# The first feed-forward stage of an eight-stage kernel as one scheduled block, with masks turned by DMA

## The reference

```python
INTER, SPARSITY, RANK = 1792, 32, 16
inter = xf @ c1_w.T @ c2_w.T                  # c1_w [16, 512], c2_w [1792, 16]
blk = inter.reshape(B * T, INTER // SPARSITY, SPARSITY)
idx = jnp.argmax(blk, axis=-1) + jnp.arange(0, INTER, SPARSITY)
h = jax.nn.relu(jnp.einsum('bkm,bm->bk', w1[idx], xf))
out = jnp.einsum('bk,bkm->bm', h, w2t[idx])
x = x + out
```

## Time and profile before

| | |
|---|---|
| median of 3 runs | 1888.47 us (1884.77 to 1889.16) |
| profiled execution | 1886.01 us, span 1884.3 us |
| granted TensorE clock, mean | 0.929 of full speed |
| PE busy | 1605.5 us (85%) |
| DVE busy | 1178.5 us (63%) |
| ACT busy | 796.8 us (42%) |
| POOL busy | 608.8 us (32%) |

### The profile page before, as it was taken

One profiled execution on the slowest core, in us unless ns is written; L12 is line 12 of the kernel. 1 busy time (PEld: TensorE's weight loads), 2 busy tenths in 40 slices (PEclk: granted clock), 3 DMA queues, 4 the chain that ended last, 5 costly groups with the idle time before them and its releaser, 6 DMA issues. The chain is left out here.

```text
span 1884.3 us, 31640 instructions
## 1 busy us (share of the span) xinstructions
PE 1605.5 (85%) x10796; PEld 897.1 (48%) x10796; DVE 1178.5 (63%) x2287; ACT 796.8 (42%) x2789; POOL 608.8 (32%) x517
## 2 busy tenths in 40 slices
PE   2888955899899999996699999999996769449997
PEld 1455532344366666652365555555552334234443
DVE  5677776434455555564588887888777879771212
ACT  2676755211044334332176666666652312251111
POOL 2333328100014443450066666666653001220000
PEclk9899976799999999998799999999999779869998
DMA  2000012000034442240264546565433000200001
GB/s 103 15 15 15 1 69 92 0 0 0 1 83 93 78 78 62 57 79 26 94 141 104 132 106 129 105 133 107 99 77 91 34 1 1 62 31 0 0 0 45
DMA packets 265956, 111.07 MB, mean 59 GB/s; under 512 B 232305, under 2 KB 248497, under 8 KB 265698
## 3 DMA queue, kind: packets, MB, share of 16 engines
q1 hardware_dynamic: 265826, 109.40, 25.1%
HBM read 52.74 MB, written 2.10 MB: 29 GB/s over the span
## 5 line engine op out<-in xcount | busy, mean ns | idle before, releaser
L67 PE MATMUL bank<-a_wo_hi,a_o_hi 128*128 128x512 f16 (+1 forms) x416 | 159.1, 382 | 19.1 <-DVE a_o_lo L824 10.4
L1443 POOL TENSOR_TENSOR a_recip<-a_total,minus_one 128x4 f32<-128x4 f32 x96 | 97.8, 1019 | 195.9 <-ACT a_probs L1295 195.9
L69 PE MATMUL bank<-a_wo_hi,a_o_lo 128*128 128x512 f16 (+1 forms) x416 | 159.1, 383 | 0.0
L68 PE MATMUL bank<-a_wo_lo,a_o_hi 128*128 128x512 f16 (+1 forms) x416 | 159.1, 382 | 0.0
L1450 POOL TENSOR_TENSOR a_normal<-a_probs,a_recip 128x512 f32<-128x512 f32 x128 | 155.4, 1224 | 7.5
L1435 POOL TENSOR_TENSOR a_q_ss<-a_q_ss,half 128x4 f32<-128x4 f32 x64 | 89.2, 1393 | 189.3 <-DVE a_q_ss L1365 95.5
L1295 ACT ACTIVATE a_probs<-a_masked,a_negmax 128x128 f32<-128x128 f32 x256 | 99.6, 390 | 94.8 <-DVE a_negmax L1340 94.8
L1306 ACT ACTIVATE a_o_hi<-bank 128x512 f16<-128x512 f32 (+1 forms) x96 | 57.1, 595 | 180.6 <-PE bank L69 180.4
L1558 ACT ACTIVATE f_h_hi<-f_h 128x512 f16<-128x512 f32 (+1 forms) x50 | 31.5, 630 | 205.8 <-DVE f_h L1579 144.1
L67 PE MATMUL bank<-xn_hi,f_w_hi 128*128 (+1 forms) x288 | 110.9, 385 | 8.2 <-PEq L1511 8.2
L437 POOL TENSOR_TENSOR a_kb_lo<-a_k_lo,a_spread 128x1024 f16<-128x1024 f16 x32 | 69.4, 2169 | 150.1 <-PE bank L69 139.5
(11 more groups left out here) (338 smaller groups left out, 4894.4 us busy)
## 6 DMA issues: line engine op xcount, KB each, us to landing
a_nq<-in_L_xattn_Wq SPq DMA_DIRECT2D x8, 1024.0 KB, 5.7
a_no<-in_L_xattn_Wo SPq DMA_DIRECT2D x8, 1024.0 KB, 6.0
f_n<-in_L_ffn_w SPq DMA_DIRECT2D x1, 3584.0 KB, 11.6
f_n<-in_L_ffn_w2t SPq DMA_DIRECT2D x1, 3584.0 KB, 20.2
a_nq<-in_L_xattn_Wq SPq DMA_DIRECT2D x4, 768.0 KB, 4.8
a_no<-in_L_xattn_Wo SPq DMA_DIRECT2D x4, 768.0 KB, 5.7
f_words<-in_L_ffn_w SPq DMA_DIRECT2D x2, 1280.0 KB, 6.0
ctx_nat<-in_ctx_t SPq DMA_DIRECT2D x4, 512.0 KB, 4.9
```

What stands on the lines that cost most here:

```text
L67: pe.matmul(out, lh, rh, start=start, stop=False)
L68: pe.matmul(out, lh, rl, start=False, stop=False)
L69: return pe.matmul(out, ll, rh, start=False, stop=stop)
L1443: pool.tensor_tensor(recip[s % 2][:, :], total[s % 2][:, :], K.minus_one[:, :], ALU.pow).then_inc(recip_done.sem, 1)
```

## The change

`top_of_blocks_ffn` and its call of `ffn` are replaced by `blocks_ffn`, one block in which all engines follow one table of steps, -16 to 29. Step t has tile t up (0 to 27) and tile t-2 down (`LAG = 2`). All is written out; there is no loop at run time. Four tables say at which step a piece is made: `NORM` (a batch normalised), `CX` (a batch compressed), `PICK` (a batch's scores chosen, in spans of four tiles) and `SPLIT` (a weight piece of two tiles split).

- The scores come in parts of 512 units (the last of each batch has 256) and are chosen between the tiles. For the first half of the tokens, span 0 is chosen at steps -7 to -4, span 1 at -1 to 2, span 2 at 3 to 6, span 3 at 7 to 10. The first tile of a span waits for its four masks.
- Masks are turned by DMA (`turn_mask`) and no longer by PE and ACT. The rows of the layer norm are split first (DVE high, POOL low) and turned by two DMAs for each batch (`turn_rows`).
- The weights are loaded and split in 14 pieces of 512 KB; two pieces of each matrix are in flight.
- `before` has -1 on its diagonal, so that its product with the mask is -1 at the winner and not below zero elsewhere. ACT makes the gate `first_f` from it by one Relu with scale -1; the DVE operation of line 1574 is gone.
- The `up`, `side`, score and compress products take turns in a ring of four banks.

```diff
+    PARTS, HT, PIECES, TILES = -(-NT // SPAN), HALF * P, NT // 2, 2 * NT
+    FIRST, LAG, RING, MASKS = -16, 2, 2, 4
+    NORM = {0: -16, 1: -15, 2: -14, 3: -13, 4: 2, 5: 3, 6: 4, 7: 5}
+    CX = {0: -9, 1: -8, 2: -7, 3: -6, 4: 4, 5: 5, 6: 6, 7: 7}
+    PICK = {(b, i): (4 * i - 5 if i else -7) + b if b < HALF else 4 * (i + 1) + b for b in range(B) for i in range(PARTS)}
+    SPLIT = {("w1", 0): -15, ("w2", 0): -10, ("w1", 1): -6, ("w2", 1): -4}
+    SPLIT.update({(kind, q): 2 * q - 4 + i for q in range(2, PIECES) for i, kind in enumerate(("w1", "w2"))})
...
             @block.sync
             def _(sp):
...
+                def turn_rows(b):
+                    sp.wait_ge(xlo_done.sem, xlo_done.count(b))
+                    for a, dst in enumerate((K.xn_hi, K.xn_lo)):
+                        sp.dma_start_transpose(dst[:, :, b * P:(b + 1) * P], xn_hl[b % HALF][:, a, :]).then_inc(xt_in[b], 16)
+
+                def turn_mask(part):
+                    b, i = part
+                    m, n = parts.index(part) % MASKS, width(part)
+                    sp.wait_ge(pick_done.sem, pick_done.count(part))
+                    sp.dma_start_transpose(mask_t[:, SPAN * i:SPAN * i + n // P, b * P:(b + 1) * P], mask[m][:, 0:n]).then_inc(mask_in[m], 16)
...
+                for t in steps:
+                    for b in at(NORM, t):
+                        turn_rows(b)
+                    for part in at(PICK, t):
+                        turn_mask(part)
+                    for kind, q in at(SPLIT, t + 3):
+                        if q:
+                            load((kind, q))
...
             @block.tensor
             def _(pe):
...
+                for t in steps:
+                    for u in live(t):
+                        up(u)
+                        first_of_block(u)
+                    for part in at(PICK, t):
+                        score(part)
+                    for b in at(CX, t):
+                        compress(b)
+                    for u in live(t - LAG):
+                        down(u)
...
             @block.scalar
             def _(act):
...
+                    for u in live(t):
+                        first_winner(u)
+                        high_of_hidden(u)
+                    for use in at(SPLIT, t):
+                        high_of_weight(use)
+                    for b in at(CX, t):
+                        high_of_compressed(b)
...
+                def choose(part):
...
+                    dve.tensor_reduce(best, s, AX.X, ALU.max).then_inc(top_done.sem, 1)
+                    dve.wait_ge(top_done.sem, top_done.count(part))
+                    dve.tensor_tensor(dst, s, best.unsqueeze(2).to_broadcast([P, width(part) // BLK, BLK]),
+                                      ALU.is_equal).then_inc(pick_done.sem, 1)
+                    dve.wait_ge(pick_done.sem, pick_done.count(part))
+                    dve.sem_inc(ring.freed(use), 1)
...
-                with dve.Fori(1, B // 2) as p:
-                    choose(2 * p, 0)
-                    choose(2 * p + 1, 1)
-        staged.close()
-        ffn(K, L, w1_p, w2_p, first_of=(mask_t, before), keep_stats=True)
...
+                    for u in live(t):
+                        hidden(u)
+                        low_of_hidden(u)
+                    for b in at(NORM, t):
+                        normalise(b)
...
+                    for b in at(CX, t):
+                        low_of_compressed(b)
+                    for part in at(PICK, t):
+                        choose(part)
```

More of the change, by code:

```diff
@@ L1714, in top_of_blocks_ffn @@
[L1714 to L1722 removed]
+        ring_of = lambda n, k, shape, dt: [sb(f"{n}{i}", shape, dt) for i in range(k)]
@@ new lines, in blocks_ffn @@
+        live = lambda t: [t] if 0 <= t < TILES else []
+        at = lambda table, t: [use for use, when in table.items() if when == t]
+        steps = range(FIRST, TILES + LAG)
+        ring_uses = [use for t in steps
+                     for use in ([(k, u) for u in live(t) for k in ("up", "side")] + [("s", part) for part in at(PICK, t)]
+                                 + [("cx", b) for b in at(CX, t)])]
+        y_bank = Banks(K, f"{N}_y", K.bank[0:4], [(hf, n) for hf in range(2) for n in range(HALF)])
@@ new lines, in blocks_ffn @@
+        ring = Banks(K, f"{N}_ring", K.bank[4:8], ring_uses)
+        in_c, w_here = sem("in_c"), {k: [sem(f"{k}_in{i}") for i in range(RING)] for k in nat}
+        pieces = sorted(SPLIT, key=SPLIT.get)
+        whi_done, wlo_done = Steps(sem("whi"), pieces), Steps(sem("wlo"), pieces)
+        mean_done, root_done, const_done, zeroed = sem("mean"), sem("root"), sem("const"), sem("zeroed")
+        chi_done, clo_done = Steps(sem("chi"), ["c1", "c2"]), Steps(sem("clo"), ["c1", "c2"])
+        per_batch = lambda n: Steps(sem(n), batches)
@@ new lines, in blocks_ffn @@
+        xn_done, xhi_done, xlo_done, cxhi_done = (per_batch(n) for n in ("xn", "xhi", "xlo", "cxhi"))
+        parts = sorted(PICK, key=PICK.get)
+        top_done, pick_done = Steps(sem("top"), parts), Steps(sem("pick"), parts)
+        xt_in, mask_in = [sem(f"xt_in{b}") for b in batches], [sem(f"mask_in{m}") for m in range(MASKS)]
+        hhi_done, hlo_done = Steps(sem("hhi"), tiles), Steps(sem("hlo"), tiles)
+        down_done = Steps(sem("down"), [u for u in tiles if u % NT < NT - 1])
+        of_half = lambda u: range(HALF * (u // NT), HALF * (u // NT) + HALF)
@@ L1723, in _ @@
             @block.tensor
             def _(pe):
[L1725 removed]
+                for banks in (y_bank, ring):
                     for freed in banks.freed_sems:
                         pe.sem_inc(freed, 1)
[L1729 to L1734 removed]
@@ new lines, in score @@
+                def score(part):
+                    b, i = part
+                    use = ("s", part)
+                    if i == 0:
+                        pe.wait_ge(clo_done.sem, clo_done.count("c2"))
+                        pe.wait_ge(ring.freed(("cx", b)), ring.n_drained(("cx", b)))
+                    pe.wait_ge(ring.freed(use), ring.n_free(use))
+                    n, first = width(part), SPAN * P * i
+                    pe.matmul(ring[use][:, 0:n], cx_s[:, b * P:(b + 1) * P], c2_s[:, first:first + n],
+                              start=True, stop=True).then_inc(ring.filled(use), 1)
@@ new lines, in first_of_block @@
+                def first_of_block(u):
+                    f, b0, use = u % NT, HALF * (u // NT), ("side", u)
+                    if f == 0:
+                        pe.wait_ge(const_done, 4)
+                    if f % SPAN == 0:
+                        for b in of_half(u):
+                            mask_landed(pe, (b, f // SPAN))
+                    pe.wait_ge(ring.freed(use), ring.n_free(use))
+                    pe.matmul(ring[use][:, :], before[:, :], mask_t[:, f, b0 * P:b0 * P + HT], start=True, stop=True).then_inc(ring.filled(use), 1)
```

386 lines of the change are left out of this document (213 added, 173 removed).

## The result

| | before | changed |
|---|---|---|
| median | 1888.18 us (4 runs, 1884.77 to 1889.16) | 1838.63 us (4 runs, 1835.29 to 1839.53) |
| ratio to before | | 0.9739 (95%: 0.9728 to 0.9751) |
| profiled execution | 1886.01 us, span 1884.3 us | 1837.94 us, span 1836.2 us |
| PE busy | 1605.5 us (85%) | 1577.1 us (86%) |
| stage, from its first DVE instruction to that of the next | 244.39 us | 196.61 us |

What follows compares the result with a forecast made beforehand. Choosing and weight splits were taken to stand on the path ahead of PE-bound products. 303.2 + 156.1 + 2.5 = 461.8 against 512.0, 50.2 us less: 1886.0 becomes 1835.8, plus 2.5 for the median, 1838 (1829 to 1846, 0.68).

Steps and rivals of the forecast that it cites:

- The opening: Second stage up to the first tile's mask matmul: forecast at 303.2 us instead of 353.1, 49.9 us earlier.
- Done for batch 0 well before, so this is hidden by the memsets: Opening: DVE's normalisation, 0.47 us a batch plus a cast, ends before POOL's clears end at 277.7 and costs nothing.
- The mark: Start of the first tile's mask matmul, from which the prediction counts the tiles: forecast 303.2 us, before 353.1.
- 1.06 each: Opening: POOL's low halves of rows, each taken as half of 2.12 us.
- The tiles: First mask matmul to last matmul: 156.1 us of PE work plus 2.5 us of waits.
- rival 2: DVE becomes the bound in steps 2 to 10: 8 to 12 us, so 1846 to 1850; chance 0.10.
- joint waits: PE's waits between the old products' 14 pairs, 10.4 us; said to go because down matmuls come two steps later.
- The rule against it: Skill page: 128x128 turn 1309 ns by DMA, 390 on TensorE; turns one by one would give near 1872.
- Rival 1: Row turns and loads get in each other's way; first mask matmul slips 5 to 12 us, 1843 to 1850; chance 0.16.
- rival 3: Slower: PE waits a little every step and its clock stays at half in the tiles, up to 1995; chance 0.02.
- Rival 4: No change: the 50 us come back behind the stage; chance 0.01.
- Rival 5: Better: shortest loads, no tile waits, cheap small operations, 2.6 + 2.5 + 2 less, 1831; chance 0.03 for below 1829.

Runs made afterwards that it cites:

- dve_memset: Changed kernel with the two tiles cleared by DVE instead of POOL: 1838.67 us, ratio 0.9734 to the kernel before.
- Lag1: Changed kernel with down matmuls one step behind the up matmuls instead of two: 1838.43 us, ratio 0.9734 to the kernel before.
- pe_more: Changed kernel plus 112 PE transposes of a constant into the score's own bank, masks still turned by DMA: 1845.50 us, ratio 0.9784 to the kernel before.
- pe_ring: Changed kernel plus 112 PE transposes of a constant into their own ring bank, copied out by ScalarE; masks by DMA: 1859.34 us, ratio 0.9859 to the kernel before.
- load_early: Changed kernel with the second w1 and w2 pieces loaded at the stage's start, ahead of the row turns: 1835.46 us, ratio 0.9725 to the kernel before.
- split_late: Changed kernel with the second w1 piece split one step later, behind the fourth batch's tokens: 1835.41 us, ratio 0.9718 to the kernel before.
- combined: Changed kernel with second weight pieces loaded early, tiles cleared by DVE, first w1 piece split at step -12: 1831.32 us, ratio 0.9706 to the kernel before.

## Why the prediction was right, step by step

**The opening, 49.9 us earlier: measured 47.3 by the stage's own clock, 47.9 by the span's.** The mark came at 305.2 (forecast 303.2), in a stage that began 0.6 sooner. The chain was the one described, and these are the terms that differ:

- *"Done for batch 0 well before, so this is hidden by the memsets"* and *POOL's "1.06 each"* were mis-sized. DVE's normalisation did not run beside the clears, it ended 277.2 instead of about 276, and a row's low half took 1.15 to 1.39, the last one 2.98. The fourth ended at 288.0 where the sum had 284.4: 3.6 late, 4.2 by the stage's clock. The largest part, 1.9, is that last one, 2.98 against 1.06; the rest is 0.7 for the normalisation, about 1.1 of waits for DVE's casts, and slightly longer operations. dve_memset shows the cause of the normalisation's length alone. The 2.98 recurs beside the same DVE operation in nine of the ten other runs, and no run moved that operation, so its cause is read from the timelines and not tested.
- That lateness did not all arrive. SP's queue of turns had been late too in the sum (last start 287.3; measured 289.26), so 2.0 were left, and the load landed in 4.1 us where the sum took 4.9 from the earlier trace rows: its split began at 294.7 against 293.5.
- From the tokens (297.55) to the third choice's end (302.12) it is 4.57 us where the sum had 4.4: choices begin 1.56 apart (297.58 and 299.14), not 1.46. And the mark comes 3.1 behind that end, not 2.5, since SP takes up a turn some 0.3 us after its choice and PE its landing as late again. That makes the last 0.8 us of the 2.0 by which the mark is late.

**The tiles, 156.1 + 2.5 = 158.6: measured 158.86.** The waits were 1.1 before tile 2 (I had 1.4) and 0.2 for later masks (1.1): 1.3, so 1.5 us lie in no wait, and no run shows where. Lag1 shows that one reason I gave was too much: the joint waits of the earlier trace rows go with a distance of one step already. DVE's margin at steps 2 to 5, the ground of rival 2, held: its 24 large reductions and comparisons take 0.687 and 0.691 in the mean, and PE has no wait there beyond the two shown.

**The median, 1838: measured 1838.63.** The agreement within 1 us is partly luck. The stage was forecast 50.2 us shorter and is 47.8 shorter, so the profiled execution came 2.1 above its forecast of 1835.8; the 2.5 that were added for the distance from that execution to the median turned out to be 0.7.

**The rule against it.** The 32 masks land 2.5 us after their issue in the median and 5.0 at the most, and PE waits 1.0 us for them in all; with TensorE's turning the stage is 19.6 us longer. The Trainium skill, "VectorE: DVE Perf Modes", section "Rules for kernel authors", says of a 128x128 transpose: "Use TensorE if PSUM dest is OK; xbar DMA otherwise". The trace agrees with its condition rather than its first half: the transposes are cheap, 0.048 us each (pe_more), but a PSUM bank for them is not free in a ring of four (pe_ring, 17.4 us).

**The rivals.** Rival 1 did not come in: the turns of rows were held up by POOL and not by one another, and the load landed at 4.1. The turns were, though, the next link behind the load (load_early, split_late). Rival 2 is out by the waits, rival 3 by the granted clock, 1.00 from the mark to the end. Rival 4 is out as well: 47.8 us of the stage arrive as 48.1 in the profiled execution, so nothing came back behind it. Rival 5's 1831 is what combined reaches, by other means than a short landing. Its 2.6 takes the 1.3 of a short landing for two loads; by the sum's own opening the first of them frees only 0.4 (280.2 against 279.8).

## What to carry to other kernels

Where one phase keeps the vector engines busy and the next keeps TensorE busy, a single table of steps can put the first under the second; count first what stays ahead of the first product, since that is all that is left (here 33 us of 81). Price a move to TensorE by the PSUM banks that it takes in the step as well as by its matmuls: here 4 us of transposes cost 17. And a queue that issues loads in the order of the schedule makes a load as late as the work queued ahead of it: either of two small edits gave back 3.9 us.

## What the runs showed of the hardware

**DVE and POOL held each other up for most of an instruction.** Beside POOL's clears DVE's normalisation took 2.68 instead of 0.54 to 0.55; its casts took 1.26 or 2.23 beside POOL's subtraction and 0.43 alone; POOL's own subtraction took 2.98 beside a two-input DVE operation, against 1.15. Each DVE operation so held up ends about 0.3 us after POOL's. Choices, which read PSUM, kept 0.69 whatever POOL did. Only the first of these was tested by a run (dve_memset); the others are read from the timelines. The Trainium skill, "SBUF — State Buffer", section "Who interferes with whom", says that DVE and GpSimd share a pair of ports, that DVE's casts and `tensor_scalar` can take it and that the other engine then blocks fully; the trace agrees, 2.68 against 0.55. By that rule the first of the terms above would have been a wait for the clears, and not nothing.

**A 512 KB load landed between 3.4 and 6.6 us after its issue** in this stage over all the runs of the new schedule, 4.0 to 4.3 in the median of each, and an issue 2 us earlier landed at nearly the same time (dve_memset). A term of that size in a sum should carry both ends.
